# A graph attention layer on one core: a ring of 30 gathered blocks instead of 36, and four places instead of three for halves of adjacency tiles

## The reference

```python
h = jnp.maximum(_layernorm(x, axis=-1), 0.0)
# graph attention on h
h = jnp.einsum('ni,hif->hnf', x, W)                 # x here is the normed input
s1 = jnp.einsum('hnf,hf->hn', h, a1)
s2 = jnp.einsum('hnf,hf->hn', h, a2)
scores = jax.nn.leaky_relu(s1[:, :, None] + s2[:, None, :], negative_slope=ALPHA)
scores = jnp.where(adj[None] > 0, scores, NEG_BIG)
att = jax.nn.softmax(scores, axis=-1)
out = jnp.einsum('hnm,hmf->hnf', att, h)            # laid out as (N, 512)
return x + jax.nn.elu(out)
```

## Time and profile before

| | |
|---|---|
| median of 3 runs | 799.62 us (799.23 to 802.81) |
| the profiled execution | 800.83 us, its span 799.0 us |
| TensorE, VectorE, ScalarE, GpSimd busy | 71%, 83%, 59%, 54% of the span |
| mean granted TensorE clock | 0.848 |
| moved by DMA | 269.5 MB, mean 337 GB/s |
| indirect gathers in the edge stage | 247, by GpSimd |
| loads of half adjacency tiles | 96, of which 33 are issued in the edge stage |

### The profile page before, as it was taken

How to read it: one execution, slowest core, us unless ns; L and a number is a source line. 1 busy time by engine, 2 the same in 40 slices (tenths; PEclk the granted TensorE clock), 3 DMA queues, 4 the chain that set the end, 5 groups by cost and what they waited for, 6 DMA issues and landing times.

```text
span 799.0 us, 9153 instructions
## 1 busy us (share of the span) xinstructions
PE 570.9 (71%) x2182; PEld 406.0 (51%) x2182; DVE 659.7 (83%) x2066; ACT 470.2 (59%) x695; POOL 427.6 (54%) x804
## 2 busy tenths in 40 slices
PE   0489788998788887653777686857476759977770
PEld 0245444554444444343556565646465648766650
DVE  4659988999876777764879999999699989999861
ACT  0778888799999899235265665657354223333321
POOL 4634444534432332237666467557467776887830
PEclk9989999999987889755888779787697679998895
DMA  9999998899999999319999999999999887999995
GB/s 288 420 356 392 359 356 346 334 396 419 415 422 418 421 421 421 138 55 343 349 373 409 402 420 385 409 399 402 396 389 281 241 254 196 269 269 276 285 256 109
DMA packets 65130, 269.51 MB, mean 337 GB/s; under 512 B 12145, under 2 KB 12145, under 8 KB 52786
## 3 DMA queue, kind: packets, MB, share of 16 engines
q1 hardware_dynamic: 38706, 190.53, 59.7%
q0 software_dynamic: 26368, 78.36, 33.0%
HBM read 243.49 MB, written 25.37 MB: 336 GB/s over the span
## 4 chain that ended last, share of the span: by engine, by line
DVE 22%; issue 11%; PE 8%; POOL 6%; DMA 6%; ACT 2%; another core or an unknown queue 2%; POOLq 0%; DVEq 0%; ACTq 0%
DVE nodes L1116 7%; DMA nodes<-table,list_column 5%; POOL nodes L959 3%; DVE places L250 3%; POOL nodes L954 2%; PE psP L1254 2%; DVE agg L1128 2%; PE psP L1255 2%; DVE best L239 2%; PE psP L1261 1%; PE psP L1262 1%; PE psC L1238 1%; ACT packed L229 1%; DVE owner L1050 1%
## 5 line engine op out<-in xcount | busy, mean ns | idle before, releaser
L651 PE MATMUL psH<-sb_W,normedT 128*128 128x512 f32 x384 | 225.5, 679 | 0.0
L229 ACT ACTIVATE packed<-adj_rows,eight 128x3072 uint8<-128x3072 int32 x66 | 188.7, 2859 | 2.1 <-issue 1.4
L954 POOL DMA_INDIRECT nodes<-table,column x138 | 139.7, 1012 | 75.7 <-issue 39.8
L1254 PE MATMUL psP<-nodes,ident 128*128 128x256 f32 x276 | 105.9, 472 | 55.0 <-issue 43.0
L959 POOL DMA_INDIRECT nodes<-table,list_column x109 | 112.0, 1027 | 58.4 <-issue 31.7
L1116 DVE TENSOR_TENSOR nodes<-nodes,psW 128x2048 f32<-128x2048 f32 (+4 forms) x66 | 138.7, 2143 | 4.2 <-ACT psW L1026 4.2
L698 POOL TENSOR_TENSOR sb_node_sum<-sb_node_sum,h_rows 128x512 f32<-128x512 f32 x48 | 61.2, 1274 | 150.9 <-ACT h_rows L616 150.9
L652 PEld LDWEIGHTS psS<-sb_Wa,normedT 128*128 128x128 f32 x384 | 78.6, 205 | 103.7 <-issue 103.7
L250 DVE FIND_INDEX8 places<-best,packed 128x8 uint32<-128x96 f32 (+6 forms) x240 | 110.5, 469 | 0.0
L239 DVE MAX8 best<-packed 128x8 f32<-128x96 f32 (+6 forms) x240 | 103.3, 463 | 6.2 <-ACT packed L229 6.1
L1255 PE MATMUL psP<-nodes,ident 128*128 128x264 f32 x276 | 102.7, 460 | 0.0
(11 more groups left out here) (177 smaller groups left out, 924.9 us busy)
## 6 DMA issues: line engine op xcount, KB each, us to landing
adj_rows<-in_adj_dram SPq DMA_DIRECT2D x66, 1536.0 KB
sb_adj_rows<-in_adj_dram SPq DMA_DIRECT2D x30, 1536.0 KB, 11.6
table<-h_rows SPq DMA_DIRECT2D x48, 260.0 KB, 7.5
sb_x_rows<-in_x_dram SPq DMA_DIRECT2D x48, 256.0 KB, 7.7
result<-in_x_dram POOLq DMA_DIRECT2D x19, 512.0 KB
out_dram<-result SPq DMA_DIRECT2D x19, 512.0 KB
result<-in_x_dram POOLq DMA_DIRECT2D x10, 256.0 KB
out_dram<-result SPq DMA_DIRECT2D x10, 256.0 KB
```

The lines of the kernel that those rows point to most:

```text
L229: nc.scalar.activation(words.bitcast(mybir.dt.uint8), sb["adj_rows"][buffer_of(i)][:], ACT.Square, bias=sb["eight"][:], scale=-17.0, accum ...
L651: nc.tensor.matmul(psH[:, t % 2], normedT[:, t % 2, kc], sb["W"][:, kc], start=(kc == 0), stop=(kc == KC - 1))
L954: nc.gpsimd.indirect_dma_start(out=nodes[:, node_at[u] + i * w.direct + j], out_offset=None, in_=table, in_offset=bass.IndirectOffsetOnAxi ...
L1254: nc.tensor.matmul(low, sb["ident"][:], nodes[:, n, 0:LOW], start=a, stop=False)
```

## The change

The ring has 30 blocks (12 KB less in each partition of SBUF), and the fourth place of the six, `adj_rows3`, is kept during the edge stage (12 KB more). So one more half (number 63) is loaded in the scan stage, and every load of the edge stage waits for the packing of the half four numbers earlier. No instruction of an engine is added or removed, and no DMA.

```diff
+LATE_BUFFERS = 4
@@ def buffer_of(i):
-    return i % 6 if i < 2 * EARLY else (i - 2 * EARLY) % 3
+    return i % 6 if i < 2 * EARLY else (i - 2 * EARLY) % LATE_BUFFERS
@@ project_and_scan, SyncE
-                for i in range(6, 2 * EARLY + 3):
+                for i in range(6, 2 * EARLY + LATE_BUFFERS):
                     if act_round[occupant(i)] == t:
                         load_adj(sp, sb, adj, i)
@@ def attend_edges(nc, sb, x, adj, table, out):
-    AHEAD, TURNS, RING, LOW = 3, 4, 36, HF // 2
+    AHEAD, TURNS, RING, LOW = 3, 4, 30, HF // 2
@@ attend_edges, SyncE
-                for i in range(2 * EARLY + 3, 2 * TILES):
-                    if max(0, act_round[i - 3 - 2 * EARLY]) == u:
+                for i in range(2 * EARLY + LATE_BUFFERS, 2 * TILES):
+                    if max(0, act_round[i - LATE_BUFFERS - 2 * EARLY]) == u:
                         load_adj(sp, sb, adj, i)
@@ def build(nc, x, adj, W, a1, a2, out):
-            for k in range(3):
+            for k in range(LATE_BUFFERS):
                 tmp(f"adj_rows{k}", [P, HALF], I32)
-                                           ("digits", [P, N], F32), ("node_sum", [P, HF], F32), ("adj_rows3", [P, HALF], I32),
+                                           ("digits", [P, N], F32), ("node_sum", [P, HF], F32),
                                            ("adj_rows4", [P, HALF], I32), ("adj_rows5", [P, HALF], I32)):
```

## The result

The changed kernel takes 813.56 us (median of 4 runs, 810.26 to 814.28) against 800.10 for the kernel before (799.23 to 802.81): a ratio of **1.0166**, 95% interval 1.013 to 1.0203, so 13.5 us slower. Two more comparisons on other chips gave 1.0162 (1.0112 to 1.0213) and 1.0149 (1.0103 to 1.0196). The forecast was 821.4 us, 21.8 us slower, with a range from 812 to 829 us.

The account below looks back on a forecast made before the run. VectorE and the DMA engines were taken as near full in the edge stage, with GpSimd's unbroken gather issue setting the end. Terms 8 - 2 + 4 + 11.8 gave +21.8 us, median 821.4 us, range 812 to 829.

Parts of the forecast that it names:

- Step 1: Unit 6 waits for unit 4's sums, so its gathers land late: +8 us; unit 5's hold is covered.
- Steps 2 and 3: Units 7 to 14 give 2 us back at unit 14's gather wait; unit 16, waiting for unit 14's sums, adds 4.
- Step 4: Unit 22 waits for unit 19's sums, so GpSimd issues everything from unit 23 on later: +11.8 us at the end.
- Step 5: Fourth place for halves: no packing waited for a half, so earlier loads end no stall: 0 us.
- (c): Edge stage: fewer and earlier loads dissolve transfer backlog and all early VectorE stalls, 2 us faster, 797.5 us; chance 0.03.
- (a): The middle is won back: unit 14's landing shortens and its 7.0 us wait goes, +16.4 us, 816.0; chance 0.26.
- (b): Transfer backlog stays or grows: unit 14 +9, unit 16 +6.1, then 11.8, median 826.5 us; chance 0.19.
- (d): The ring wait isn't there because sums end early enough; without the last chain's step alone, 809.6 us; chance 0.05.
- The price of a gather: Skill's rule for GpSimd DMAs: 2.6 us per gather, unit 6 2 us late, unit 16 not at all, sum about 14.
- another end of the scan stage: Sign against the prediction: the scan stage itself ending at another time than 335 us.

Follow-up runs that it names:

- 36 blocks laid out: The kernel before with its 36 ring blocks placed by a hand-written list instead of the program's rule, three places: 795.93 us, ratio 1.0007.
- 32 blocks by the rule: The kernel before with a ring of 32 blocks placed by the program's own rule and four places for halves: 816.74 us, ratio 1.0182.
- 30 blocks laid out: The changed kernel, four places, with its 30 ring blocks placed by a hand-written list that loses no remainder: 807.37 us, ratio 1.0184.
- 32 laid out without a remainder: The changed kernel's four places with a ring of 32 blocks placed by a hand-written list: 798.22 us, ratio 1.0058.

## Why the prediction was right, and where it was off

The direction, the order of size and the mechanism behind unit 5 were right, and the time fell inside the range, near its lower end. Two things in that were luck: unit 6's terms missed in opposite directions, and a gain of 7.6 us that the prediction didn't have kept the total in the lower half of the range. Point by point:

- **Step 1, unit 6: +8.** Unit 6 comes 20.9 us after unit 5 instead of 12.2 (means): +8.7. The release by unit 4's sums and the 0.8 us were as put. But the sum came earlier against VectorE than put: unit 6's first gather starts 2.05 us ahead of unit 5's first score in all three profiles, where the forecast had it 0.4 us behind. And the landing took longer: the last gather starts at 444.34 and unit 6 is scored at 455.20, 10.9 us later (11.9 and 11.6 in the other two), not 8.8. The two misses cancel. Part of the +8.7 isn't the hold's either: 36 blocks laid out, without the early loss and without a hold at unit 6, take 13.9 us and wait 1.59 there.
- **Steps 2 and 3: -2 and +4.** From unit 6 to unit 16 it is +0.4 us (144.9 to 144.5). Their net of +2 lies within what this stretch does by itself. Where VectorE waits differs by the execution: in the first profile 3.99 us at unit 14 (7.0 before) and 2.73 at unit 16, in the second 1.12 at unit 15 and 0.51 at 16, in the third 7.14 at unit 15. The wait of GpSimd before unit 16 was 18.95 us long. So the forecast wait at unit 16 itself came in one profile of three.
- **Step 4, the last chain: +11.8.** Unit 22 is released by unit 19's sum at 665.12 + 0.8, unit 23 follows 12.1 us later, and 16 to 22 takes 1.5 us more, 22 to the end 8.7 more: +10.2, 1.6 us less than forecast. VectorE waits it off at once, at units 22 to 24: 9.9 us in the first profile (1.69 + 2.93 + 5.29), 10.0 and 9.9 in the others.
- **Step 5, the fourth place: 0.** The packing has no wait, and with three places the stretch behind unit 5 is the same (376.9). Its reason, that no packing waits for a load, holds for the first profile; in the second a packing waits 1.6 us for one. Two places are too few (11.4 us of waits).
- Together, from unit 5 on: +21.8 forecast, **+19.2** measured.

**The step that failed is in step 1: it took the stretch up to unit 5 as unchanged.** I costed unit 5's hold at nothing, since 15 us covered it, and left out of the list that units 3 and 4 wait one unit later as well (unit 3 for unit 0, where it waited for none, and unit 4 for unit 1 and not 0). The three holds are 2.70, 2.99 and 2.88 us long (unit 5's first gather starts 4.0 us later, counted from the first gather of all, where the forecast had 11), and no VectorE wait comes from them. But the kernel before loses 7.6 us just there, and the changed kernel doesn't. The signs are in the earlier trace rows: a wait of 4.2 us for the exponential and one of 2.2 us for nothing that the profile shows. The largest stall stands behind them, on ScalarE. It copies what TensorE has looked up for unit 4 (L1002). In the first profile of the kernel before the look-up ends at 384.34 + 0.86 = 385.20, and the copy starts at 396.60. Then come two packings, which the program puts ahead of the exponential, and that is what VectorE waits for:

```profile
384.34 0.86 PE L1238 MATMUL psC<-infoB,owner 128*128 128x42 f32 x6 [0.17 <-issue]
396.60 0.28 ACT L1002 ACTIVATE facts<-psC 128x126 f32<-128x126 f32 x1 [12.20 <-remote]
```

In the changed kernel the copy starts 0.14 us after the look-up's end:

```profile
386.24 0.86 PE L1239 MATMUL psC<-infoB,owner 128*128 128x42 f32 x6 [0.93 <-issue]
387.25 0.28 ACT L1003 ACTIVATE facts<-psC 128x126 f32<-128x126 f32 x1 [0.95 <-PE psC L1239]
```

This parts all fourteen profiles: 9.3 to 17.0 us lie between the two in the seven that have 93 us or more up to unit 5, and 0.04 to 0.14 us in the seven that have 86. The profile names nothing that ends the wait ("remote"). TensorE's own matmuls of unit 1 come one at a time from 393 us on, with nothing to wait for:

```profile
391.19 1.09 PE L1262 MATMUL psP<-nodes,to_row 128*128 128x264 f32 x2
392.07 0.86 PE L1261 MATMUL psP<-nodes,to_row 128*128 128x256 f32 x2
393.53 0.38 PE L1262 MATMUL psP<-nodes,to_row 128*128 128x264 f32 x1 [0.59 <-issue]
394.93 0.38 PE L1262 MATMUL psP<-nodes,to_row 128*128 128x264 f32 x1 [1.02 <-issue]
396.35 1.01 PE L1254 MATMUL psP<-nodes,ident 128*128 128x256 f32 x2 [1.04 <-issue]
```

In the changed kernel the same stretch runs through, and VectorE has one wait from 370 to 430 us, unit 0's:

```profile
393.44 1.08 PE L1263 MATMUL psP<-nodes,to_row 128*128 128x264 f32 x2
394.32 1.06 PE L1262 MATMUL psP<-nodes,to_row 128*128 128x256 f32 x2
395.17 1.08 PE L1263 MATMUL psP<-nodes,to_row 128*128 128x264 f32 x2
```
```profile
DVE score L1096 <- DMA nodes<-table,list_column: 9.8, 1, 9.8
```

I had these stalls as part of rival (c), at 6.4 us, but let them go only together with all others and only by relief of the transfers. They went alone, and took 7.6 us with them. 19.2 - 7.6 + 0.6 (the first gather starts that much later in the mean) is 12.2 us by the profiles, beside 13.5 by the medians.

Why they go stays open. In the first comparison and on two further chips, the changed kernel has 86 in 3 of 3 profiles, and kernels with 32 to 42 blocks have 93.4 or more in 7 of 7. On one more chip all four kernels had 86, one with 36 blocks too. So something of the chip or the moment decides whether there is a loss, and where there is one, 30 blocks by the rule are without it. The fourth place alone doesn't take it away: the kernel with 32 blocks by the rule has it too, lays units 0 to 6 into the same blocks as the kernel before, and loses the whole of it (93.4) on the chip where the changed kernel has 86.2. Whether the small ring does so without the fourth place wasn't tried on such a chip. That holding units 3 and 4 for a few us thins out the transfers is argued only. Unit 3's place doesn't decide it, nor does moving TensorE's instructions by 16. A late supply of instructions to ScalarE, which stands still longest, wasn't tried and isn't excluded.

**The rivals.** (a), the middle won back, gave 816.0 and is nearest in time, but mostly by another route: in the first profile unit 14 gave back 3.0 us of its 7.0, in the second all of them, and in the third unit 15 waited 7.14 instead. (b) didn't happen: the landing at unit 14 got shorter, not longer (17.84 us instead of 25.86). (d) had it that without step 4 10 us would be left. No run has the other two holds without that of unit 22, but two come near, and they show that the holds of units 16 and 22 aren't to be priced apart. From unit 16 to the end the change costs 10.2 us. 32 blocks by the rule, held at unit 16 and not at 22, take 8.3 us more there than the kernel before; 30 blocks laid out, held at unit 22 and not at 16 (but some us each at 17 to 19), take 6.6 more. Together that is more than both cost at once. So the sum of 21.8 came out near because it took unit 19's last sum as its start and counted GpSimd's lateness once; (d) took the whole of step 4 away with unit 22's hold, where these runs say that most of it stays.

**The price of a gather.** By the Trainium skill, page "DMA: Bandwidth & Descriptors", section "Anatomy of one DMA — SWDGE (gpsimd) path", I had an estimate of 2.6 us for a gather of 266 KB. It gave a sum of about 14, near the measured total; but the landings, 10.9 to 11.9 us after the start of unit 6's last gather and 6.06 of unit 32's in the changed kernel, and the 19.2 us behind unit 5 go against it. Its total is near by coincidence with the early 7.6 us.

## What to carry to other kernels

For a ring buffer, write down for each user which earlier user it waits for, before and after: the size in blocks says little, the remainder lost at the wrap and jumps from the third to the second before decide (30 blocks lost 19 us behind unit 5, 32 by the rule about 15, 32 laid out without a remainder 2 to 3, or 0.6% by the runs' times). Look at every unit of the list: the 22.58 us at unit 7 were expected to be under 5. A producer that issues without a pause to the end, as GpSimd here, doesn't make up a hold in the middle, so price such holds by the lead that they take together, once, and don't add them. And before costing a stretch at "unchanged", look whether the first profile has stalls in it that nothing explains: follow each back to the first engine that stands still, take a second profile, and count them as something that can go.

## What the runs showed beside that

- The edge stage starts at 344.0 to 349.6 us in ten of the fourteen profiles and at 353.8 to 355.2 in four, which have three or four places and 30 to 36 blocks. The kernel before (36 and three) starts at 347 us, so neither number decides it. Three of the four ran on one chip, whose fourth kernel starts at 346.4; the last (32 by the rule) ran on the chip where the kernel before starts at 347.9. It is a difference of some 10 us that no part of the change explains, and larger than most effects here. The prediction named another end of the scan stage as a sign of being wrong; against this spread the changed kernel's start, 0.6 us later in the mean, can't be told from the same. Only the cut at events of the trace made the rest comparable.
- With its queue empty and loads beside it, unit 6's ten gathers had landed 9.9 us after the end of its last gather's issue (455.20 - 445.29); unit 16's, when few loads were left, 4.2 us after (600.47 - 596.30).
- A packing that never waits with four places for halves, and 0 to 2.7 us in all with three, waits 11.4 us with two: the step from enough to too few is one place wide.
